# Fourteen pieces given banks in the two score rings, the order of pieces and of stack transfers re-drawn, in a two-layer transformer kernel on one core

## What is computed

```python
x = x + attention0(layernorm(x))      # 16 heads of 8, biases, softmax(q k^T / sqrt(8)) v, then wo
x = x + gated_mlp(layernorm(x))       # silu(x wg^T) * (x wu^T), 384 hidden, then wd^T
x = x + attention1(layernorm(x))      # 16 heads of 8, rms norm on q and k
x = x + base_and_lora(layernorm(x))   # x W^T + b, and 8 experts of rank 8, mixed by a softmax router
```

## Time and profile before

| what | value |
|---|---|
| median of 3 executions | 2010.79 us (2009.87 to 2018.42) |
| the profiled execution, its own time | 2036.95 us |
| its span, first to last instruction | 2035.1 us |
| PE busy | 1781.7 us (88%) |
| DVE busy | 1604.8 us (79%) |
| ACT busy | 1430.6 us (70%) |
| POOL busy | 437.4 us (21%) |
| mean granted TensorE clock | 0.942 of 2.4 GHz |

### The profile page before, as it was taken

One profiled execution on the slowest core, in us unless ns is written; L12 is line 12 of the kernel. 1 busy time (PEld: TensorE's weight loads), 2 busy tenths in 40 slices (PEclk: granted clock), 3 DMA queues, 4 the chain that ended last, 5 costly groups with the idle time before them and its releaser, 6 DMA issues.

```text
span 2035.1 us, 32181 instructions
## 1 busy us (share of the span) xinstructions
PE 1781.7 (88%) x10958; PEld 654.2 (32%) x10958; DVE 1604.8 (79%) x3587; ACT 1430.6 (70%) x2921; POOL 437.4 (21%) x579
## 2 busy tenths in 40 slices
PE   4998998989989898898989989898898989899895
PEld 1232332323333232333323233232332323333233
DVE  3978786877888879887877978789688887887981
ACT  2777676776777868776776867768577676676773
POOL 3122112131122223112121212223022131122201
PEclk8899997998999999998989989899799998999997
DMA  6223405032050412405042050422405032032210
GB/s 120 59 70 83 97 24 136 18 111 54 24 142 18 118 42 68 102 24 136 24 111 49 29 136 18 111 49 64 106 13 147 18 88 71 18 80 64 80 34 22
DMA packets 162644, 141.34 MB, mean 69 GB/s; under 512 B 38761, under 2 KB 144050, under 8 KB 162482
## 3 DMA queue, kind: packets, MB, share of 16 engines
q1 hardware_dynamic: 162482, 139.29, 26.6%
HBM read 77.38 MB, written 55.57 MB: 65 GB/s over the span
## 4 chain that ended last, share of the span: by engine, by line
PE 38%; DVE 22%; DMA 14%; ACT 11%; issue 6%; SPq 5%; POOL 4%; DVEq 0%; ACTq 0%; POOLq 0%
DVE neg_max L911 14%; PE ps L1205 12%; PE ps L1190 7%; ACT probs L707 6%; PE ps L1226 6%; DMA k_stack<-k_rows 4%; PE ps L1180 3%; DMA rden_all<-rden_rows 3%; DMA q_stack<-m_parts 3%; DMA k_rows<-kp 3%; PE ps L1143 2%; ACT xn L713 2%; PE ps L1270 2%; PE ps L1231 2%; SPq L441 2%
## 5 line engine op out<-in xcount | busy, mean ns | idle before, releaser
L911 DVE TENSOR_REDUCE neg_max<-ps 128x1 f32<-128x512 f32 x2048 | 1317.9, 682 | 219.4 <-PE ps L1180 214.7
L707 ACT ACTIVATE probs<-ps 128x512 f32<-128x512 f32 x2048 | 1098.8, 596 | 374.9 <-PE ps L1190 374.2
L1180 PE MATMUL ps<-k_stack,q_stack 48*128 48x512 bf16 x2048 | 709.5, 403 | 83.2 <-DMA k_stack<-k_rows 45.2
L1190 PE MATMUL ps<-q_stack,k_stack 50*128 50x512 bf16 x2048 | 682.9, 399 | 78.0 <-ACT probs L707 37.1
L1205 PE MATMUL ps<-probs,v_aug 128*32 128x512 f32 x4096 | 576.2, 636 | 0.1
L1190 PEld LDWEIGHTS ps<-q_stack,k_stack 50*128 50x128 bf16 x2048 | 154.1, 95 | 628.5 <-ACT probs L707 384.0
L1180 PEld LDWEIGHTS ps<-k_stack,q_stack 48*128 48x128 bf16 x2048 | 158.2, 95 | 223.2 <-DVE neg_max L911 158.4
L606 POOL TENSOR_TENSOR o_raw<-o_raw,rden_all 128x512 f32<-128x512 f32 x64 | 81.3, 1271 | 660.6 <-DMA rden_all<-rden_rows 660.4
L1205 PEld LDWEIGHTS ps<-probs,v_aug 128*32 128x32 f32 x4096 | 82.1, 110 | 160.8 <-issue 96.5
L587 POOL TENSOR_TENSOR rstd<-vpe,half_neg 128x4 f32<-128x4 f32 x64 | 64.4, 1007 | 304.3 <-DVE vpe L902 304.3
L713 ACT ACTIVATE xn<-x,shift,rstd 128x128 f32<-128x128 f32 x192 | 81.1, 491 | 32.2 <-POOL shift L589 32.2
(11 more groups left out here) (103 smaller groups left out, 1521.2 us busy)
## 6 DMA issues: line engine op xcount, KB each, us to landing
q_stack<-q_rows SPq DMA_DIRECT2D x128, 192.0 KB, 3.8
k_stack<-k_rows SPq DMA_DIRECT2D x128, 192.0 KB, 4.9
rden_all<-rden_rows SPq DMA_DIRECT2D x64, 256.0 KB
q_rows<-qp SPq DMA_DIRECT2D x32, 384.0 KB, 2.6
k_rows<-kp SPq DMA_DIRECT2D x32, 384.0 KB, 3.5
q_rows<-qp SPq DMA_DIRECT2D x32, 256.0 KB, 3.0
k_rows<-kp SPq DMA_DIRECT2D x32, 256.0 KB, 3.2
x_in<-in_L_attn_x SPq DMA_DIRECT2D x16, 256.0 KB, 2.9
```

The source lines that it names most:

```text
L707: act.activation(probs[:, g % RING, :], home("score", (l, b, u)), ACT.Exp).then_inc(exps, 1)
L911: dve.tensor_reduce(neg_max[l][:, pair // 2, col:col + 1], home("max", (l, b, n)), AX.X, ALU.max, negate=True).then_inc(max_taken, 1)
L1180: pe.matmul(home("max", (l, b, m)), q_stack[l][row:row + KROWS, pair, tok:tok + 128], k_stack[l][row:row + KROWS, pair, :], start=True, st ...
L1190: pe.matmul(home("score", (l, b, u)), k_stack[l][row:row + AROWS, pair, tok:tok + 128], q_stack[l][row:row + AROWS, pair, :], start=True, ...
```

## The change

Three things are edited, all in tables and constants; no instruction of the program is added or left out.

1. **Banks.** `A_PIECES` gains `qt`, `kt`, `xt1`, `xt2`, `xt3` (readers on ACT), `V_PIECES`, empty before, gets `qka`, `qkb`, `v0`, `v1`, `pr0`, `dn` (readers on DVE). With `u0` to `u2` that is fourteen kinds in the rings of scores and maxima. Bank 7 keeps `m0` to `m3`, `xt0`, `q0`, `k0`, `g0` to `g2`, `pr1`, `rt`, `ct`, `out`.
2. **SP's order.** In the steady part `half0_p0` moves from 56 to 62, so behind `rows0` (59) and `rden0` (now 58); `out_p0` moves from 41 to 44 and `rows3` from 46 to 42, so `rows3` is issued first; `lx` goes behind `rden0` and `rows0`. `out_p1` (14 to 23), `rows2` (23 to 26) and the halves of layer 1 (32 to 35) keep their order among themselves, and `half1_p0` (66 to 70) stays ahead of `den1` and `rows1`.
3. **Places on the other engines.** PE: `q0` 3 to 0, `v1` 29 to 24 (now ahead of `m2` at 25), `ct` 64 to 61, `v0` and `m1` of the odd slot one unit earlier, `u0` with `g1` at 81, `u1` with `g2` at 84, `qkb` with `qka` at 102. POOL: `r1_q1` goes ahead of `normalise` of half 1, `r2_q1` ahead of `r1_k1`; `nf3` ahead of `r2_q0`; `um2` and `nf2` keep their order. ACT: `part1_k0` from 31 to 25, ahead of `part1_q0` (now 30); `xn0b` from 105 to 123. DVE: `gm0` from 77 to 79, `tv1` from 29 to 24, `inv0` from 50 to 43 and from 114 to 107, the Newton steps `nw1` to `nw13` later.

```diff
--- before.py
+++ after.py
@@ -43,52 +43,52 @@
 
 PARTS_OF = {"q0": 2, "k0": 2, "v0": 2, "v1": 2, "rt": 2, "pr0": 4, "pr1": 4, "dn": 4, "out": 4, "qka": 2, "qkb": 2,
             "g0": 2, "u0": 2, "g1": 2, "u1": 2, "g2": 2, "u2": 2}
-PE_AT = {"A": {"m0": -7, "m1": 9, "m2": 25, "m3": 41},
-         "P0": {"xt0": -2, "q0": 3, "k0": 12},
-         "P0_fast": {"xt0": 3, "q0": 5, "k0": 7},
-         "V0": {"v0": 16},
-         "M1": {"pr0": 19, "xt1": 27, "g0": 29, "u0": 31, "g1": 33, "u1": 35, "g2": 37, "u2": 39, "dn": 43,
-                "xt2": 51, "qka": 54, "qkb": 55},
-         "M2": {"qt": 16, "kt": 19, "v1": 30},
-         "E": {"pr1": 22, "xt3": 40, "rt": 44, "ct": 64, "out": 69}}
+PE_AT = {"A": {"m0": -7, "m1": 8, "m2": 25, "m3": 41},
+         "P0": {"xt0": -3, "q0": 0, "k0": 13},
+         "P0_fast": {"xt0": 4, "q0": 6, "k0": 9},
+         "V0": {"v0": 15},
+         "M1": {"pr0": 19, "xt1": 27, "g0": 29, "u0": 33, "g1": 33, "u1": 36, "g2": 36, "u2": 39, "dn": 44,
+                "xt2": 51, "qka": 54, "qkb": 54},
+         "M2": {"qt": 16, "kt": 20, "v1": 26},
+         "E": {"pr1": 22, "xt3": 40, "rt": 45, "ct": 61, "out": 69}}
 ACT_AT = {"A": {"save0": 36, "save1": 67},
-          "P0": {"part0_q0": 10, "part0_k0": 14, "part1_q0": 27, "part1_k0": 31},
-          "P0_fast": {"part0_q0": 7, "part0_k0": 8, "part1_q0": 13, "part1_k0": 14},
-          "S0": {"xn0a": 39, "xn0b": 41},
-          "M1": {"xn1": 25, "xn2": 48, "sq0": 54, "sq1": 56},
-          "M2": {"part0_q1": 17, "part0_k1": 20, "part1_q1": 20, "part1_k1": 22},
-          "E": {"xn3a": 35, "xn3b": 36, "gexp": 52}}
-DVE_AT = {"A": {"inv0": 50, "inv1": 73},
-          "S0": {"st0a": 24, "st0b": 27, "mo0": 27, "fa0": 32},
-          "V0": {"tv0a": 16, "tv0b": 16},
-          "M1": {"add0": 19, "st1": 20, "mo1": 20, "gm0": 29, "gm1": 33, "gm2": 37, "down": 43, "st2": 44,
-                "mo2": 45, "tqa": 54, "tqb": 55, "nw0": 55, "nw1": 57, "nw2": 59, "nw3": 60, "nw4": 61,
-                "nw5": 62, "nw6": 63, "nw7": 64, "nw8": 67, "nw9": 71, "nw10": 72, "nw11": 73, "nw12": 74,
-                "nw13": 75},
-          "M2": {"tv1a": 30, "tv1b": 30},
-          "E": {"add1": 22, "st3a": 23, "st3b": 23, "mo3": 27, "fa3": 28, "ro0": 44, "ro1": 45, "ro2": 52,
-                "ga0": 53, "ga1": 55, "ga2": 56, "fin": 69}}
+          "P0": {"part0_q0": 7, "part0_k0": 16, "part1_q0": 30, "part1_k0": 25},
+          "P0_fast": {"part0_q0": 6, "part0_k0": 11, "part1_q0": 14, "part1_k0": 16},
+          "S0": {"xn0a": 44, "xn0b": 59},
+          "M1": {"xn1": 24, "xn2": 49, "sq0": 54, "sq1": 56},
+          "M2": {"part0_q1": 17, "part0_k1": 21, "part1_q1": 20, "part1_k1": 22},
+          "E": {"xn3a": 35, "xn3b": 38, "gexp": 49}}
+DVE_AT = {"A": {"inv0": 43, "inv1": 72},
+          "S0": {"st0a": 25, "st0b": 27, "mo0": 33, "fa0": 35},
+          "V0": {"tv0a": 15, "tv0b": 15},
+          "M1": {"add0": 19, "st1": 20, "mo1": 20, "gm0": 31, "gm1": 34, "gm2": 37, "down": 44, "st2": 45,
+                "mo2": 45, "tqa": 54, "tqb": 54, "nw0": 55, "nw1": 61, "nw2": 64, "nw3": 65, "nw4": 65,
+                "nw5": 67, "nw6": 69, "nw7": 72, "nw8": 73, "nw9": 74, "nw10": 74, "nw11": 75, "nw12": 76,
+                "nw13": 76},
+          "M2": {"tv1a": 26, "tv1b": 26},
+          "E": {"add1": 22, "st3a": 22, "st3b": 26, "mo3": 27, "fa3": 28, "ro0": 45, "ro1": 47, "ro2": 49,
+                "ga0": 52, "ga1": 54, "ga2": 56, "fin": 69}}
 POOL_AT = {"A": {"no0": 53, "no1": 74},
-           "S0": {"nf0": 39},
-           "P0": {"r1_q0": 23, "r1_k0": 24, "r2_q0": 34, "r2_k0": 41},
-           "P0_fast": {"r1_q0": 6, "r2_q0": 12, "r1_k0": 10, "r2_k0": 22},
-           "M1": {"nf1": 24, "um0": 27, "um1": 29, "um2": 40, "nf2": 50},
-           "M2": {"sc0": 7, "sc1": 7, "r1_q1": 11, "r2_q1": 22, "r1_k1": 19, "r2_k1": 22},
-           "E": {"nf3": 45, "mix": 52}}
-SP_AT = {"A": {"rows0": -5, "rows1": 10, "rows2": 23, "rows3": 46, "den0": 40, "rden0": 55, "den1": 66,
-                "rden1": 74},
-         "P0": {"out_p0": 41, "half0_p0": 56, "half1_p0": 66},
-         "P0_fast": {"out_p0": 21, "half0_p0": 31, "half1_p0": 63},
-         "S0": {"lx": -9},
-         "M1": {"lr0": 59},
-         "M2": {"out_p1": 15},
-         "H1": {"cpx2": 13, "half0_p1": 32, "half1_p1": 32},
-         "H1_tail": {"cpx2": 18, "half0_p1": 34, "half1_p1": 64},
-         "E": {"store": 69}}
+           "S0": {"nf0": 42},
+           "P0": {"r1_q0": 23, "r1_k0": 32, "r2_q0": 39, "r2_k0": 44},
+           "P0_fast": {"r1_q0": 8, "r2_q0": 18, "r1_k0": 17, "r2_k0": 18},
+           "M1": {"nf1": 25, "um0": 27, "um1": 28, "um2": 52, "nf2": 53},
+           "M2": {"sc0": 6, "sc1": 6, "r1_q1": 11, "r2_q1": 17, "r1_k1": 22, "r2_k1": 25},
+           "E": {"nf3": 36, "mix": 44}}
+SP_AT = {"A": {"rows0": -5, "rows1": 10, "rows2": 26, "rows3": 42, "den0": 40, "rden0": 58, "den1": 70,
+                "rden1": 76},
+         "P0": {"out_p0": 44, "half0_p0": 62, "half1_p0": 70},
+         "P0_fast": {"out_p0": 18, "half0_p0": 33, "half1_p0": 67},
+         "S0": {"lx": -3},
+         "M1": {"lr0": 57},
+         "M2": {"out_p1": 25},
+         "H1": {"cpx2": 17, "half0_p1": 35, "half1_p1": 35},
+         "H1_tail": {"cpx2": 41, "half0_p1": 30, "half1_p1": 62},
+         "E": {"store": 77}}
 
 
 M1_EARLY = -16
-M2_EARLY = -1
+M2_EARLY = -2
 GROUPS = []
 for n, (layer, b) in enumerate(ATTENDS):
     GROUPS.append(("A", (layer, b), n, 0))
@@ -145,8 +145,8 @@
     return (*ATTENDS[n], t % UNITS) if 0 <= n < LAST else None
 
 
-A_PIECES = ("u0", "u1", "u2")
-V_PIECES = ()
+A_PIECES = ('u0', 'u1', 'u2', 'qt', 'kt', 'xt2', 'xt3', 'xt1')
+V_PIECES = ('qka', 'qkb', 'v1', 'pr0', 'v0', 'dn')
 A_RING, V_RING, PIECE_RING = (0, 1, 2), (3, 4, 5), (7,)
```

## The result

The changed kernel takes 1888.67 us (median of four, 1882.22 to 1890.93) against 2014.61 us for the kernel before on the same chip: a ratio of 0.934, 95% interval 0.929 to 0.939. It is faster, by about twice what was forecast (1951 us), and outside the range of 1915 to 2003. The profiled execution took 1890.93 us, for a span of 1889.1.

A forecast was written before the change was run, and what follows sets the result against it. No engine was saturated; waits keeping PE and DVE, the heaviest engine, apart bound the kernel. Terms -21 - 25 - 9 - 5 + 16 = -44, with 15 for the clock, took the median 2010.8 to 1951 us; range 1915 to 2003.

The forecast's parts named there:

- (a): Layer 1's stack, awaited at unit 38: POOL's new order brings it 1.3 us earlier per entry; 21 us gained.
- (b): Maxima rows, awaited at unit 64: `rows0` issued ahead of the stack's DMAs; 25 of 31.0 us gained.
- (f): Granted clock, falling behind the waits at units 38 and 64: 40 us gained in the profile, about 15 for the median.
- (c): Bank 7 with eleven kinds fewer: 9 us of waits gained, and 5 us from `gm0` at 79.
- (d): Pieces lodged in rings of three: scores or maxima behind wait for a younger read; 16 us lost, about 0.09 each.
- (e): Waits moved by `inv0`, `part1_k0`, `rows3`, `xn0b`: DVE does not stall; cost nothing, at worst 1 us x 16.
- Waits go but the clock stays: Rival, chance 0.18: waits go, but the clock or the stack's wait at unit 38 stays; 1988 us.
- DVE paces everything: Rival, chance 0.06: DVE sets the pace, only the maxima rows' gain is felt, half taken back; within 10 us of 2011.
- The rings couple PE to its readers: Rival, chance 0.13: each lodging costs a third of a us or more; at 0.5 us, 2039 us.

The follow-up runs named there:

- the fill: Kernel before with PE's idle time in the two DMA waits (units 38 and 64) filled with matmuls nobody reads: 1986.83 us, ratio 0.987.
- the three edits: Kernel before with SP's new table, the new lodging and the two POOL numbers together, other places as before: 1931.02 us, ratio 0.957.

## Why the prediction was wrong

That the DMA waits shrink and the clock rises with them was found, with sizes too small; what the lodging was worth was not found. Against the profiled execution the prediction had 1953 us and the execution took 1891, 62 us less. The shares below are of the profiled executions: the DMA waits as measured, the clock by the 0.39 us of the fill, an estimate, and what is left.

- **(a) and (b), the DMA waits: 46 forecast, 60 measured** (45.2 - 15.9 and 31.0 - 0.6). (b) came out whole rather than at 25, though SP's table is only one of two edits that remove it. (a) was mis-sized: the stack's path got 2.9 us shorter, landing at 30.4 us of the pair in place of 33.4, where the step said 1.3. The step let the residual come forward by 1.15 us, which in the earlier trace rows is the residual's own length, and counted 0.7. In truth its input was there at 914.2, when this copy ended, so that the order alone was worth 1.9 us (the residual started at 916.08):

```profile
913.51 0.67 ACT L688 ACTIVATE qp<-qf 128x512 bf16<-128x512 f32 x1
```

It started 3.2 us earlier in the pair (medians), the rest because ACT reads `qt` 1.5 us sooner. The 0.6 us for a free queue was about right: from the first issue to the last landing k's DMAs took 3.4 us, before 4.1. The step also said that the wait would stay because PE, too, comes sooner to unit 38; PE came only 0.5 us sooner (30.3 against 30.8).
- **(f), the clock: 40 forecast in the profile, some 54 measured** (11.6 us less at the lower level in each of twelve pairs, 0.39 us each). The step took half of the 75.5 us, since the first of the two waits would go and the second only shrink. With a mean wait of 0.3 us at unit 38 the clock fell there in one pair of the twelve, behind the one wait of over 1 us (1.5). For the median the step then took only 15 us. Its premise, that the other executions had less time at the lower level, is right: their mean clock was 0.957, against 0.942. The term was too small even so: by the recorded clocks (0.957 to 0.980, 172 to 75 us at the lower level) it is 38 us at 0.39, an estimate, and the fill alone gave 29.
- **(c) and (d), the lodging and the pieces' places: 2 us lost forecast, about 32 gained** (146 - 60 - 54, what is left over; PE's waits other than for DMA fell by 30). This is the step that failed most. (d)'s 16 us of loss did not show: with the pieces' own waits, PE waits 71 us for the readers, before 70. Under the old places it did, in part: there these waits rose from 70 to 81 us, against some 16 us of waits for bank 7 that went, and the lodging by itself gave 6 us. So (c) and (d) were near the truth for the old order of work. They priced the banks by the waits for bank 7 in the kernel *before*. Under the new places the lodging is worth 62 to 66 us, because pieces had been put side by side that would have waited for one another. Its worth lay in the arrangement that it permits, and the trace of before has no row for that. (The 62 is more than the 32, since part of it only keeps away waits that the new places would have brought.)
- **(e)** held as far as `inv0` goes: DVE did not stall at it, and the inverse, now early, lets the next stack out earlier, which the step had not looked for.
- **The rivals.** Waits go but the clock stays: no, as the windows at 1.00 show. DVE paces everything: no. The rings couple PE to its readers, with the clock falling behind: no run shows it; the lodging alone, the kernel in which it would stand by itself, has 11 us more of such waits than the kernel before, 0.07 for each lodging where the rival needs 0.34, and the same clock (0.955 and 0.958 in the mean). The page of the Trainium skill that was named for it (TensorE: Matmul & The Clock Gate, "A second HAM failure mode: psum-queue depth-cycling") describes a clock that oscillates over frequent, very short idles. Most stretches with such idles ran at the upper level here, but not all: of the 2.3 us a pair that the changed kernel still spends at the lower one, 2.0 begin at unit 99, in six of the twelve pairs, behind a wait of 0.73 us for DVE at unit 97. The mean wait at unit 119 is as long, and no fall stands there. Where the wait at unit 97 was cut to 0.3 us (`pr0` and `dn` in halves), the falls at 99 were gone. To that extent a short idle did pull the clock down here, for an estimated 0.8 us a pair (2.0 us at 0.39).

What stays open: how the 42 us between the three edits and the changed kernel share out among the single places on PE, ACT and DVE, and whether `inv0` alone would remove the wait at unit 64. A number of `PE_AT` does more, too, than the sentence on units says ("changes the order on one engine and nothing else"): it also moves the piece's turn in its ring, and so its bank and the read that PE waits for.

## What to carry to other kernels

A wait of PE for a DMA has two prices, the idle time and the lower clock behind it; by estimate the second was nearly as large as the first in the profiled executions (54 us to 60), and less in the medians. The two small edits gave about a third more than the waits for DMA that they removed: SP's table 33 us for 26, POOL's two numbers 47 for 34. Look for transfers that could start earlier in the order of the engines that feed the queue: two numbers in POOL's order gave 47 us. Buffers and the order of work are to be priced together: extra banks were worth 6 us in the old order and 62 in the order that used them, and a wait that two edits can each remove is counted once (SP's table: 33 us by itself, 9 beside the other edits).

## What the runs showed of the hardware

Filling PE's idle time with 17 useless matmuls per pair (3.6 us by the estimate on record) made the kernel 29 us faster (2016.3 to 1986.8). The granted clock rose from 0.94 to 0.98 in the steady part of the profiled executions, from 0.957 to 0.973 in the mean of all. Time at the lower of the two levels cost 0.39 to 0.45 us for each us, estimates from the profiled executions and from the medians, less than the half that PE would lose if it alone set the pace. DMAs of 4 KB (`rows0`), issued behind four of 192 KB on the same queue, held PE until 5.5 us after their issue where the last of the four landed 5.1 us after it; where it landed 2.6 us after it, they were in time for PE, which came 3.8 us after it (medians of twelve pairs). In the steady part of the kernel before, the recorded falls of the clock at units 38 and 64 begin 1.4 to 5.0 us after PE began to wait, behind waits of 1.5 to 3.6 us; in the changed kernel six follow a wait of 0.73 us (unit 97).
